# Attention stage whose first rows are normalised and turned in the stage before it, with the key bias summed on VectorE

## What is computed

```python
x = x + tanh(g_ffn[0])   * L0_ffn(layernorm(x), qweight, wparams, bias)     # int8-quantised
x = x + tanh(g_xattn[1]) * L1_xattn(layernorm(x), ctx_4096, Wq, bq, Wk, bk) # plain attention

def L1_xattn(text, features, Wq, bq, Wk, bk):
    Q = text @ Wq.T + bq                  # 112 x 1024 per batch
    K = features @ Wk.T + bk              # 375 x 1024 per batch
    attn = softmax(Q @ K.T / sqrt(1024))
    return attn @ features
```

## Time and profile before

| | us |
|---|---|
| median of three runs | 2812.06 |
| profiled execution, its own time | 2815.97 |
| its span | 2814.3 |
| PE busy | 2584.0 (92%) |
| DVE busy | 1898.8 (67%) |
| ACT busy | 1080.5 (38%) |
| POOL busy | 553.1 (20%) |

### The profile page before, as it was taken

How to read it: one execution, slowest core, us unless ns; L and a number is a source line. 1 busy time by engine, 2 the same in 40 slices (tenths; PEclk the granted TensorE clock), 3 DMA queues, 4 the chain that set the end, 5 groups by cost and what they waited for, 6 DMA issues and landing times. The chain is left out here.

```text
span 2814.3 us, 48289 instructions
## 1 busy us (share of the span) xinstructions
PE 2584.0 (92%) x18264; PEld 1841.8 (65%) x18268; DVE 1898.8 (67%) x3366; ACT 1080.5 (38%) x2605; POOL 553.1 (20%) x602
## 2 busy tenths in 40 slices
PE   7999999999999699998899999998788999878898
PEld 5856855855865488886555555655487788556664
DVE  6376376376467577774578877777558889867774
ACT  3443434334335233332334444443355655302221
POOL 0110100001012100000045554455223333200000
PEclk9999999999999899998899999998899999989998
DMA  8011010101113845556275666544250010544521
GB/s 325 2 38 58 3 59 23 38 25 58 37 47 82 278 115 140 157 149 220 103 246 165 180 172 172 161 127 118 63 201 9 24 47 24 141 142 169 176 98 33
DMA packets 155491, 311.31 MB, mean 111 GB/s; under 512 B 84112, under 2 KB 107312, under 8 KB 145768
## 3 DMA queue, kind: packets, MB, share of 16 engines
q1 hardware_dynamic: 128952, 232.78, 25.8%
q0 software_dynamic: 20384, 60.82, 7.3%
q10 hardware_dynamic: 5936, 14.75, 1.8%
HBM read 249.53 MB, written 42.52 MB: 104 GB/s over the span
## 5 line engine op out<-in xcount | busy, mean ns | idle before, releaser
L1765 DVE TENSOR_REDUCE latent_nmax<-bank 112x1 f32<-112x487 f32 x128 | 85.0, 665 | 242.9 <-PE bank L1568 236.5
L1460 POOL TENSOR_SCALAR latent_probs<-latent_probs,latent_rsum 112x487 f32<-112x487 f32 x128 | 89.0, 709 | 786.0 <-DVE latent_rsum L1770 786.0
L2197 POOL TENSOR_SCALAR grouped_probs<-grouped_probs,grouped_rsum 112x375 f32<-112x375 f32 x256 | 169.8, 682 | 280.5 <-DVE grouped_rsum L2253 280.4
L2464 PE MATMUL bank<-ffn_qT,gather_whole 128*128 128x128 bf16 x3584 | 207.0, 220 | 16.7 <-ACT ffn_us L2587 6.7
L2464 PEld LDWEIGHTS bank<-ffn_qT,gather_whole 128*128 128x128 fp8e4 x3584 | 203.0, 98 | 21.6 <-issue 20.3
L2647 POOL TENSOR_TENSOR ffn_h<-ffn_sl,ffn_us 128x512 f32<-128x512 f32 x56 | 126.8, 2265 | 278.6 <-ACTq L2590 278.6
L2144 ACT ACTIVATE grouped_probs<-bank,grouped_nmax 112x375 f32<-112x375 f32 x256 | 143.3, 572 | 76.0 <-DVE grouped_nmax L2249 76.0
L2249 DVE TENSOR_REDUCE grouped_nmax<-bank 112x1 f32<-112x375 f32 x256 | 122.3, 540 | 73.4 <-PE bank L2055 71.1
L2947 PEld LDWEIGHTS bank<-gather_part,points_onehot 123*128 123x128 bf16 x3072 | 109.2, 101 | 60.9 <-DVE points_onehot L3095 30.8
L2064 PEld LDWEIGHTS bank<-const_ident,grouped_probs 112*125 112x125 f32 x768 | 105.4, 196 | 66.4 <-DVE grouped_probsT L2261 28.8
L2191 POOL TENSOR_SCALAR grouped_raw<-grouped_raw,grouped_rscale 128x1024 f32<-128x1024 f32 x96 | 119.9, 1270 | 144.7 <-DVEq L2227 144.5
(11 more groups left out here) (435 smaller groups left out, 5561.7 us busy)
## 6 DMA issues: line engine op xcount, KB each, us to landing
grouped_raw<-L_weights SPq DMA_DIRECT2D x24, 2048.0 KB, 8.9
points_spread<-numbers SPq DMA_DIRECT2D x16, 912.0 KB
codes<-grouped_flip SPq DMA_DIRECT2D x24, 512.0 KB, 2.6
front_cT<-ctxT SPq DMA_DIRECT2D x8, 1500.0 KB, 6.8
plain_ctxT<-ctxT POOLq DMA_DIRECT2D x8, 1500.0 KB, 22.2
plain_ctx<-ctx POOLq DMA_DIRECT2D x8, 1500.0 KB, 23.5
grouped_ctx<-ctxT SPq DMA_DIRECT2D x8, 1500.0 KB, 6.8
gather_whole<-numbers SPq DMA_DIRECT2D x12, 912.0 KB
```

What stands on the lines that cost most here:

```text
L2197: pool.tensor_scalar(pr[:, g % 2, j, :], pr[:, g % 2, j, :], rsum[:, g % 2, j:j + 1], 1.0, ALU.mult, ALU.mult)\
L2464: mm = pe.matmul(ahead.tile(t)[:, i * P:(i + 1) * P], wgu[:, u0 + f // 4, c:c + 2 * P - 1:2], qT[:, k, :], start=(k == 0), stop=(k == KC - 1))
```

## The change

The norm, the transposes and the copies of the first pair's rows move into `quantised_ffn`. SP copies batches 0 and 1 from the finished tiles in the core's own memory into `z` with three DMAs (112, 16 and 96 rows), where it waited for two stores and loaded them; it no longer waits for the seven stores at the end of the stage, but SP, POOL and ACT do so in the next stage. DVE does the norm behind `finished(4)`, PE the transposes behind its last matmul, ACT the roots and copies behind its last copy.

The key bias is computed another way. `Q . bk` is `z . (Wq bk) + bq . bk`. Once, at the head of the stage, DVE takes eight `tensor_tensor_reduce` of 128 x 1024 (the eight blocks of wq times the bias as a row of 1024, loaded by a new 512 KB broadcast DMA of POOL), a product and a row sum for `bq . bk`; PE spreads the nine columns over 112 partitions with nine matmuls between the second and the third piece of the first qT; DVE evicts them behind its first search. Then two `tensor_tensor_reduce` of 112 x 1024 for each pair (`summed`) give the bias of its rows: of pair 0 behind the first batch's searches, of pair p + 1 behind its norm. SP's reload of z waits for `summed` too. The sixteen one-column matmuls of each pair and the two copies of DVE go.

The last search of the second batch of each pair is split: its first half (`sort_near`) runs behind the row maximum of the first batch, its second half (`sort_far`) behind the first copy of the turned probabilities. The loop over pairs on PE and DVE is written out four times.

The core of the diff:

```diff
@@ stream_ahead
                 sp.wait_ge(*z_used(s, p))
+                sp.wait_ge(*z_summed(s, p))
                 sp.dma_start(z[:, s, :], x_in[p * 2 + (s + 2)]).then_inc(z_loaded[s], 16)
@@ class PlainRows
+    def copied(self, eng, x):
+        eng.dma_start(self.z[:, 0], x[0][0:Q]).then_inc(self.z_loaded[0], 16)
+        eng.dma_start(self.z[0:P - Q, 1], x[0][Q:P]).then_inc(self.part_copied, 16)
+        eng.dma_start(self.z[P - Q:Q, 1], x[1][0:2 * Q - P]).then_inc(self.z_loaded[1], 16)
@@ quantised_ffn
                 sp.wait_ge(x_done, b + 1)
-                sp.dma_start(x_out[b], x[b]).then_inc(x_stored, 16)
                 if b == 1:
-                    sp.wait_ge(x_stored, 32)
-                    ahead.load(sp, "z")
-            sp.wait_ge(x_stored, 16 * TILES)
+                    begun.copied(sp, x)
+                sp.dma_start(x_out[b], x[b]).then_inc(begun.x_stored, 16)
@@ vector
                 finished(b)
+                if b == TILES - 3:
+                    dve.wait_ge(begun.part_copied, 16)
+                    begun.norm.in_place(dve, begun.z, begun.z_loaded, 0, begun.z_ready)
@@ tensor
+            for s in range(2):
+                pe.wait_ge(begun.z_ready, s + 1)
+                turn_rows(pe, C, turns, begun.z[:, s], "zT", s, 0)
@@ scalar
+            for s in range(2):
+                begun.norm.root(act, s, s)
+            for s in range(2):
+                copy_turned(act, turns, begun.zT[:, s], "zT", s, 0, begun.zT_ready)
@@ plain_attention, gpsimd
+            pool.dma_start(key_row, rows(A["L1_xattn_bk_row"], P)).then_inc(key_row_loaded, 16)
+            pool.wait_ge(begun.x_stored, 16 * TILES)
@@ tensor
+            def keys_spread():
+                pe.wait_ge(products_ready, 1)
+                for i in range(3):
...
+                        mm = pe.matmul(spread.tile(t)[0:Q, j * P:(j + 1) * P], key_products[:, k:k + 1].broadcast_to([P, Q]), C.ident[:],
+                                       start=True, stop=True)
...
+                        if spreading and i == 2:
+                            keys_spread()
...
-                    for k in range(KC):
-                        mm = pe.matmul(now.tile(t)[0:Q, 400:401], qT[:, s, k, :], bk[:, k:k + 1], start=(k == 0),
-                                       stop=(k == KC - 1))
@@ scalar
-            for s in range(2):
-                norm.root(act, s, s)
-            for s in range(2):
-                copy_turned(act, first, zT[:, s], "zT", s, 0, zT_ready)
+            act.wait_ge(begun.x_stored, 16 * TILES)
@@ vector
-            norm.in_place(dve, z, z_loaded, 0, z_ready)
+            dve.wait_ge(wq_loaded, 16)
+            dve.wait_ge(key_row_loaded, 16)
+            for k in range(KC):
+                dve.tensor_tensor_reduce(out=row_product, in0=wq[:, k, :], in1=key_row, scale=1.0, scalar=0.0, op0=ALU.mult, op1=ALU.add,
+                                         accum_out=key_products[:, k:k + 1])
+                dve.drain()
+            dve.wait_ge(b_loaded, 32)
+            dve.tensor_tensor(bk[:], bk[:], bq[:], ALU.mult)
+            dve.drain()
+            dve.tensor_reduce(key_products[:, KC:KC + 1], bk[:], AX, ALU.add)
+            dve.drain().then_inc(products_ready, 1)
...
+            def summed(p):
+                for s in range(2):
+                    dve.tensor_tensor_reduce(out=z_product, in0=z[:, s, :], in1=spread_keys[:], scale=1.0, scalar=0.0, op0=ALU.mult, op1=ALU.add,
+                                             accum_out=qbk[:, p % 2, s, :])
...
-                    for i in range(3):
+                    for i in range(3 - s):
                         points.sort(dve, p * 2 + s, s, i, (3 * s + i) % 2)
+                        if p == 0 and s == 0 and i == 0:
+                            keys_spread()
+                    if s == 0 and p == 0:
+                        summed(0)
                     if s == 0 and not last:
                         norm.in_place(dve, z, z_loaded, p + 1, z_ready)
+                        dve.drain()
+                        summed(p + 1)
...
-                    dve.tensor_copy(qbk[:, s, :], now.tile(t)[0:Q, 400:401])
...
+                    if s == 0:
+                        points.sort_near(dve, p * 2 + 1, 2, 1)
...
+                    if s == 0:
+                        points.sort_far(dve, p * 2 + 1, 2, 1)
```

More of the change, by code:

```diff
@@ L519, in sort, with sort_near @@
     def sort(self, dve, b, slot, i, k):
+        self.sort_near(dve, b, i, k)
+        self.sort_far(dve, b, i, k)
+    def sort_near(self, dve, b, i, k):
         n = len(self.tiles)
@@ L533, in sort, with sort_far @@
         dve.drain()
+    def sort_far(self, dve, b, i, k):
+        n = len(self.tiles)
+        far, top = self.work[k][:, 1], self.top
         dve.max(top[:, 1, :], far)
@@ L563, in divide, with quantised_ffn @@
     dve.drain()
[L566 removed]
+def quantised_ffn(nc, C, banks, x_out, front, ahead, begun):
     x_out = token_tiles(x_out)
@@ L697, in project, with plain_attention @@
         mm.then_inc(turns.full(t), 1)
-def plain_attention(nc, C, banks, gate, x_in, x_out, A, nearest, early, ahead, rise):
+def plain_attention(nc, C, banks, gate, x_in, x_out, A, nearest, early, ahead, rise, begun):
     SCALE = float(D) ** -0.5
@@ L731, in plain_attention @@
         result = [(("o", s, h), 4 * s + h) for s in range(2) for h in range(2)]
-        first = Turns(banks, rows_turned, 1)
+        spread = Turns(banks, [(("keys", i), (0, 1, 4)[i]) for i in range(3)], 1)
         turns = Turns(banks, scored + rows_turned + result, PAIRS - 1)
@@ L793, in pair @@
                     for k in range(KC):
[L794 to L798 removed]
+                        mm = pe.matmul(now.tile(t)[0:Q, 0:CTX], tT[:, s, k, :], cT[:, s, k, :], start=(k == 0), stop=(k == KC - 1))
                     mm.then_inc(now.full(t), 1)
@@ L943, in pair @@
                     dve.drain().then_inc(ctx_free[s], 1)
-            every_pair(dve, pair)
+            for p in range(PAIRS):
+                pair(p, p == PAIRS - 1)
 def memory_ffn(nc, C, banks, gate, x_in, x_out, A, early, rise, ahead):
```

81 lines of the change are left out of this document (57 added, 24 removed).

## The result

The changed kernel takes 2823.61 us (median of 18 runs) against 2814.51 us of the kernel before on the same chip: a ratio of 1.0029, with a 95% interval of 1.0018 to 1.0040. That is 8 us by the ratio and 9.1 between the medians. The interval lies above 1, so the kernel is slower, by less than the 0.5% that was called no change in the prediction; 2823.61 is inside the range of 2803 to 2833. The forecast was 2821. Two of the executions behind the ratios of this document, one of 3082 us and one of 7701 us, were in a slower state and are left out of them.

The account below looks back on a forecast made before the run. PE filled 92% of the span, with DVE and ACT nearly as full; DVE's chain would set pair 0. Pairs 0 to 3 at +13.4, 0, -2.6 and -1.8 gave +9.0 on the median 2812.06: 2821 us, range 2803 to 2833.

Parts of the forecast that it names:

- The handover: Between feed-forward and attention: the stage opens when it did but with z turned, so the first projection starts 9 us earlier.
- The row of keys: Head of the stage: DVE waits for the new row, issue 0.5 us and landing 4, bounds 3.15 and 6.2.
- The multiply-and-sum: DVE's products and sums over 1024 elements: 1.40 us each, bounds 1.30 and 1.6.
- Rival A: DVE's products and sums: the multiply-and-sum runs at half rate, 2.5 us each, giving 2839 us; chance 0.14.
- The spread of the keys: First qT of pair 0: PE waits 2.3 us for the products, then nine small matmuls take 1.7 us.
- The reload of z: Pair 0, behind summed(0): issue 0.4 us and landing 4 before the norm can start.
- The mechanism of pair 0: DVE's late fourth search holds ACT's evictions; PE idles 17 us, scores come 12.1 later, lower clock costs 2.0.
- The charge for a dip ahead of each result: Pairs 0 to 2: PE's 1.1 us wait before the second transposes brings the lower clock, 1.1 us each, bounds 0 and 1.7.
- Steady pairs: Pairs 1, 2 and 3 against before: 0, -2.6 and -1.8 us; pairs 1 and 2 take 75.7 us each.
- The tail: From a pair's first scores to the next projection: 24.45 us instead of 26.2, 1.8 less.
- The code written out: Pair loop unrolled on PE and DVE: adds nothing that could be priced, charged 0.
- Rival B: Pair 0: the handover's gain survives because PE alone sets the scores, 3.8 us early, giving 2803 us; chance 0.14.

Follow-up runs that it names:

- early_sum: Changed kernel with summed(0) moved from behind the third search to behind the first: ratio 1.0008 to the kernel before.
- act_order: Changed kernel with ACT's squares for each pair's last search issued behind the last eviction of tT: ratio 1.0021 to the kernel before.
- no_split: Changed kernel with each pair's last search whole again, all six searches ahead of the softmax: ratio 1.0064 to the kernel before.
- row_early: Changed kernel with the row of keys loaded in the feed-forward into a buffer of its own: ratio 1.0032 to the kernel before.
- best3: Changed kernel with earlier row, bias and points loads, four products in the feed-forward, earlier sum, second slot's points begun later, ACT's squares reordered: ratio 0.9980 to before.
- handover_only: Kernel before with the handover alone; key bias by narrow matmuls, all six searches ahead of the softmax: ratio 1.0005 to the kernel before.
- split_only: Kernel before with only the split of the last search added: ratio 0.9996 to the kernel before.
- pe_points: bias_by_pe with the first points' loads ahead of the biases' in POOL's queue: ratio 1.0001 to the kernel before.
- bias_by_pe: Changed kernel with the key bias as one-column matmuls again and no SP wait for sums; handover and split kept: ratio 1.0008 to before.

## Why the prediction was right

The path that the prediction names is the one that the traces show: DVE's chain through the row of keys, the products, the searches and the reload of z, and behind it ACT's evictions, set pair 0. The size is right by luck in part. The sum, +9.0, came out as +8.5 because two errors cancelled: pair 0 cost 3.9 us more than was predicted, the other pairs gave 4.4 more back.

- **The handover.** Predicted 9 us, measured 8.5. The copies of z landed as taken, with 2.62 us of wait for the 2.6 given; the last tile ended at mark 42.2 for 41.2, and the stage opened 0.6 us sooner behind it than was taken, so that the projection began at 44.0 for 43.6.
- **The row of keys: mis-sized.** Taken at 4 us behind an issue of 0.5, between bounds of 3.15 and 6.2, since the queue was POOL's own. It took 7.9 with its issue, beyond both bounds. The products began at mark 52.1 for 48.1. The row does not land alone: x, the biases, the points and the context are issued within 6 us behind it. But the same issues stand behind it in early_sum, act_order and no_split, where it took 5.2, 4.8 and 5.5, inside the bounds; why it took longest in the changed kernel's trace is not shown.
- **The multiply-and-sum: right.** Taken at 1.40, measured 1.35 (1.23 us, and a read-out of the sum that is an instruction of its own, 0.08 us). Rival A falls. The group of these sums in the changed kernel stands beside the search's combination:

```profile
L946 DVE CUSTOM_DVE_ANT_0 plain_tT<-plain_wq,plain_tT 128x1024 bf16<-128x1024 f32 x8 | 9.8, 1226 | 10.7 <-DMA plain_tT<-L_xattn_bk_row 9.9
```

  The rule of the Trainium skill (Vector Engine (DVE) Microarchitecture Reference, "Points that are easy to get wrong"), that the scalar-tensor-tensor form with two non-bf16 SBUF sources halves throughput for want of a port for the accumulator, would have given some 2.5 us, an estimate from the search's row. The profile calls the instruction CUSTOM_DVE_ANT_0, so whether it has that form is not shown. But with the accumulator it takes 1226 ns for 1024 elements, and the search's scalar-tensor-tensor takes 1225 without one, also from two fp32 tiles in SBUF: neither runs at half rate, and the measurement decides.
- **The spread of the keys: mis-sized, without effect.** Nine small matmuls were put at 1.7 us by the step of a projection's matmul; they took 4.18 us, in 18 rows, at a granted clock of 0.55 (985 to 990), and 2.13 in row_early, where PE did not wait ahead of them and the clock was 1.00. PE waited 5.48 us for the products, not 2.3. All this lies inside PE's later 17 us, so it cost nothing.
- **The reload of z: mis-sized.** Issue and landing were taken at 4.4 us and measured at 6.3 (1016.19 to 1022.52), with 0.35 more for the second tile; the upper bound was nearer. The fourth search started 5.4 us later than predicted by the marks, and the scores came at 121.0 for 116.0.
- **The mechanism of pair 0: right.** PE waited for ACT, and act_order and early_sum show the chain by experiment. That the wait was 17.05 us where 17 were predicted is luck: PE was done with tT at mark 104.0 for 99.2 and the scores came 5.0 us late, so both ends moved by the same 5. The lower clock behind the wait cost 2.3 us (12.64 for 10.37), for 2.0.
- **The charge for a dip ahead of each result: wrong.** PE did wait, 1.20 us, ahead of the second transposes, as predicted for 1.1. But the results of pairs 0 to 2 took 10.46 to 10.47 us and the granted clock stayed at 1.00 (1059 to 1070). The 3 x 1.1 us had been taken from pair 2 of before, where a wait of 1.18 us had been followed by 11.30. The same length of wait had no dip behind it here. With 3.02 and 4.03 us (act_order) or 2.56 and 4.03 (best3) ahead of the result the dip is there, 11.59 and 11.68.
- **Steady pairs.** Predicted 0, -2.6 and -1.8; measured -2.3, -4.9 and -1.7. The missing dip is 1.1 in each of pairs 1 and 2. The scores of pair 1 were put 0.7 us late, but the fourth search started 37.4 us after the pair's first projection (1069.32 to 1106.71) where 38.5 had been taken, and its end held nothing up. The tail took 24.13 us from the scores to the next projection (24.45 predicted, though the terms as given add to 24.35). The removed matmuls were mis-sized too: from the scores to the first transposes it took 13.28 us before and takes 10.21 now, 3.1 less, where 2.7 were taken. A pair keeps 2.3 of these 3.1; most of the rest is PE's wait of 1.2 us for the second transposes. The code written out, charged with nothing, gives about 0.2 us a pair: pair 1 of handover_only, with the work of before, takes 75.54 for 75.72.
- **Rival B**, the gain survives: its end, 2803, did not occur, but best3 shows what it needed: stage 357.5, 9.4 us under before. It loads the row, the biases and the points earlier, takes half of the products off the head of DVE's chain, puts the sum ahead of two searches so that z is reloaded beside them, and alters ACT's order.

Pair 0 with the opening: +17.3 for +13.4; the others: -8.8 for -4.4.

## What to carry to other kernels

When a handover lets one engine start sooner, ask what the engine that sets the next wait needs for its first instruction, and where those loads stand; here 8.5 us of PE's head start were worth nothing, since DVE's first search waited for the points or the products. A buffer that is read by a new consumer gets a new earliest time for its reload: put that consumer where other work of the engine hides the landing (5.5 us here for moving one call). Removing matmuls that take a few us from a nearly full PE paid here only because the engine that took them over had its own slack made first, by the split. And where one trace is read against another, compare a landing that no edit touched: 2 to 3 us of difference there came by themselves.

## What the runs showed of the hardware

- A load that was issued earlier here did not land as much earlier when others were under way. From issue to first use z's reload took 6.3, 6.9, 7.8 and 10.5 us (changed, no_split, act_order, row_early). In all four the reload of the points was issued 1.2 us ahead of it; the 1500 KB of the context landed 1.1 us before z's issue in the first, and 1.8, 2.7 and 11.5 us after it in the others. The two rise together; no run changes the context alone.
- The points made DVE wait 19.8 us with z's reload beside them (handover_only), and 1.14 in best3, where z's reload came behind the first search; there the points were also issued first, and DVE was at its products until 973.8, so how much of that is the reload's absence was not separated.
- The same load, with the same issues around it, took 4.8 to 7.9 us from issue to first use in four traces (the row of keys).
- The multiply-and-sum with an accumulator shows as two instructions, 1.23 and 0.08 us, and the next one starts after 1.35.
- Matmuls with a broadcast column as weights and 128 moving columns, fp32, show as two rows each; nine took 4.18 us at a granted clock of 0.55 and 2.13 at 1.00 (row_early).
- What stays open: why the same wait of 1.2 us was followed by the lower clock in pair 2 of before (0.73 between 1193 and 1197) and not in the changed kernel. The traces divide by the one-column matmuls ahead of the wait. With them, every such wait has a longer result behind it: 1.18 us (11.30) and 0.98 with 0.46 (12.16) in before, and in the last pair 1.60 in split_only and pe_points (11.77, 11.59), 1.61 in bias_by_pe (12.92), 1.31 with 0.32 in handover_only (13.11). Without them, neither 1.20 (pairs 0 to 2 of the changed kernel) nor 2.18 us (pair 0 of no_split, 10.47) has; waits from 2.6 us on have. Most of the former are in the last pair, and no run has the same wait with and without these matmuls, so that they are the cause is not shown.
